# A graph network's edge counts: four fixed one-hots of a step from one interleaved comparison

## The chip, the cores and the metric

One core of one Trainium2 chip. The metric is the device time of one execution, in microseconds.

## The reference, cut to what matters

Four graph layers over 1250 nodes and 40000 edges, with 512 features. Each layer gathers features of source nodes and sums them per destination. The first one is

```python
i, j = edge_index[0], edge_index[1]
agg = jax.ops.segment_sum(x[j], i, num_segments=x.shape[0])
h = (1.0 + eps) * x + agg
h = jax.nn.relu(h @ W1.T + b1)
```

The others are attention over the edges (softmax per destination), a weighted message layer and a mean layer. All of them use the same edges, so the kernel turns the edge list once into dense 1250 x 1250 matrices: how often an edge joins two nodes, and the sums of the edge weights (in three bfloat16 parts). This is the edge build.

## The kernel before, in words

**Edges.** The sorted edges lie as 320 chunks of 125 (one edge per partition). `dst_oh` holds for every chunk a stationary matrix 125 x 128, bfloat16: 32 columns of one-hots of (quarter of the source, place in a window of eight destinations), and three copies of them times the weight's parts. It is made once, by 32 comparisons (L1164) and three multiplications of 10240 values by a repeated row (L1194). The moving matrix of a step is a one-hot of the source within its quarter: 313 columns, made on VectorE and multiplied on TensorE (L620); the products add up in PSUM.

**Groups.** There are 160 half windows `h` of eight destinations, four to a group `w`, so 40 groups; a group has four PSUM banks, and two groups alternate. Every half window gets FIX = 2 fixed steps per group, and in between as many late steps as its edges need: a hardware loop on VectorE and on TensorE whose count and first chunk come from a table (`groups_of`, L300: register loads, once per LOADS = 4 groups, on each of the two engines). The table gives group 0 a long loop and most of the later groups one trip.

**VectorE (L1232 to L1260).** Per group: `fixed(w, 0)`, the late loop, `fixed(w, 1)`. Each fixed call makes four one-hots (L1237), each a tensor_scalar comparison of `iota` (314 values, float16) with one float32 key per partition, and counts `base_oh` after each. Fixed slots of two groups alternate; it waits for `base_used` of the group two back. A late comparison (L1255) has one slot per half window and waits for `late_used` of the trip before.

**TensorE (L611 to L640).** Per group: four fixed products `base(0, h)`, each behind its own `base_oh`; the late loop, four products a trip; four of `base(1, h)`. Before a group it waits until ScalarE has evicted the group two back (`win_free`).

**ScalarE (L1593 to L1606)** copies each pair of banks into one of four window buffers in X, and in between computes degrees (L1584), the scaled features and, after window 50, `high_part(0)`, the rounded part of feature block 0 (L1591). **SP** stores each window with two DMAs (L398) and loads finished tiles of the counts back (L407, L409); it issues in order. The last windows come behind the loads of tiles before them.

**GpSimd (L1814 to L1836).** It clears the gaps of the window buffers, then makes `h_lo[0]`, the low part of feature block 0 (L1820, nine tiles in one tensor_tensor and the tenth in another), as soon as ScalarE's high part is there. Behind it come clears for the heavy rows (L1824 to L1827), which wait for all fixed products, and gathers (L1831), which wait for row numbers from VectorE (L1287).

**After the build** TensorE multiplies the features by the counts (L682, `aggregate`): per tile six products, three with the high and three with the low part. Tile t of block 0 waits for the counts of tile t; the loop starts behind `h_pool` 3, GpSimd's low part. VectorE makes the low parts of the other blocks (L1268).

Tiles share memory: the fixed and late one-hots lie in HT from word 0, `h_lo[0]` in HT from 3200 to 4480.

Of the kernel before, what the change touches and what calls it, by code (L numbers as in the profile page):

```python
# [19 lines left out]
F16 = mybir.dt.float16  # L20
BF16 = mybir.dt.bfloat16
# [3 lines left out]
P = 128  # L25
N, D, E = 1250, 512, 40000
T = -(-N // P)
# [7 lines left out]
FIX = 2  # L35
# [52 lines left out]
def rows(t):  # L88
    return min(P, N - t * P)


def constants():
    k1 = np.zeros((P, NK1 + 2 * NW + NH), np.float32)
    k1[:, K_IDENT:K_IDENT + P] = np.eye(P)
    for h in range(2):
        k1[:, K_TLO + h] = np.arange(P) * WIN + h * SUB
        k1[:, K_THI + h] = np.arange(P) * WIN + h * SUB + SUB - 1
    k1[:, K_ONES:K_ONES + P] = 1.0
    for k in range(3):
        for q in range(FIX):  # L100
            k1[:, K_PICK + k * FIX + q] = np.arange(P) + k * P - q
    k2 = np.zeros((NW, NK2), np.float32)
    k2[:, K2_UP:K2_UP + NC] = np.arange(NC) + 1
    k2[:, K2_DOWN:K2_DOWN + NC] = NC - np.arange(NC)
    k2[:, K2_TRI:K2_TRI + NW] = np.triu(np.ones((NW, NW)))
    k1[:, NK1:NK1 + 2 * NW] = np.arange(2 * NW) * KEY
    kh = k1[:, NK1 + 2 * NW:]
    kh[:, H_TRI:H_TRI + P] = np.triu(np.ones((P, P)), 1)
    kh[:, H_BEFORE:H_BEFORE + T * T] = np.tril(np.ones((T, T)), -1).reshape(-1)
    kh[:, H_SLOT:H_SLOT + SLOTS_H] = np.arange(SLOTS_H) + 1  # L110
    kh[:, H_ROW:H_ROW + T] = np.arange(P)[:, None] + np.arange(T) * P - OUTSIDE
    kh[:, H_OFF:H_OFF + 4] = np.arange(4) * T * P + OUTSIDE
    kh[:, H_OFF + 4] = OUTSIDE
    iota = np.broadcast_to(np.arange(HOT, dtype=np.float16), (P, HOT)).copy()
    return k1, k2, iota


def build(nc, A, out):
# [7 lines left out]
    with ExitStack() as ctx:  # L126
# [5 lines left out]
        def sem(name):  # L132
            if name not in sems:
                sems[name] = ctx.enter_context(nc.semaphore(name))
            return sems[name]
# [85 lines left out]
        epsI = BC[:, 1536:1536 + P]  # L221
        late_oh = src_oh[:, 2 * BASES:, :]
        winbuf = [X[:, :, :].rearrange("p t o -> p (t o)")[:, q * GH * PITCH:(q + 1) * GH * PITCH] for q in range(WB_N)]
        key_base = HT[:, 4860:4860 + 2 * NW]
# [24 lines left out]
        KC = [min(P, NC - k * P) for k in range(3)]  # L249
        base_key = BC[0:EC, W0:W0 + FIX * 2 * NW].rearrange("p (q v) -> p q v", q=FIX)  # L250

# [72 lines left out]

        def base_slot(w, i):
            return w % 2 * BASES + i

        def build_bank(w):
# [32 lines left out]
        def _(sp):  # L361
# [19 lines left out]
            load_last_x("x_in2")  # L381
            sp.dma_start(iota, A["iota"]).then_inc(sem("x_in"), 16)
            sp.dma_start(key_base, A["k1"][:, NK1:NK1 + 2 * NW]).then_inc(sem("x_in"), 16)
# [3 lines left out]
            for k in range(2):  # L387
                sp.dma_start(bias_col[:, 7 + k:8 + k], A["L2_bm"][k * P:(k + 1) * P].rearrange("(p o) -> p o", o=1))\
                    .then_inc(sem("x_in"), 16)

            def move_window(w):
# [123 lines left out]
        def _(pe):  # L515
# [95 lines left out]
            for w in range(NG):  # L611
# [10 lines left out]
                def base(q, h):  # L622
                    i = q * GH + h
                    pe.wait_ge(sem("base_oh"), BASES * w + i + 1)
                    step(h, dst_oh[0:EC, :, fixed_chunk(d[h], n0, q)][:, :, 0], src_oh[:, base_slot(w, i), 0:QUART],
                         q == 0).then_inc(sem("base_used"), 1)
# [59 lines left out]
            pe.wait_ge(sem("win_free"), NW - 2)  # L686
            pe.wait_ge(sem("h_pool"), 3)
            for t in range(T - 1):
                pe.wait_ge(sem("c_in%d" % (t % 2)), 32 * (t // 2 + 1))
                aggregate(0, t)  # L690
# [414 lines left out]
        def _(dve):  # L1105
# [100 lines left out]
            dve.wait_ge(sem("setup_ps"), 8)  # L1206
            dve.wait_ge(sem("x_in"), 7 * 16)
            for q in range(FIX):
# [23 lines left out]
            def fixed(w, q):  # L1232
                if w >= 2:
                    dve.wait_ge(sem("base_used"), BASES * (w - 2) + (q + 1) * GH)
                for h in range(GH):
                    v = GH * w + h
                    ve.tensor_scalar(src_oh[:, base_slot(w, q * GH + h), :], iota[0:EC, :], base_key[:, q, v:v + 1], None,  # L1237
                                     ALU.is_equal).then_inc(sem("base_oh"), 1)

# [32 lines left out]
            dve.wait_ge(sem("deg"), T)  # L1272
            dve.wait_ge(sem("x_in"), 8 * 16)
            link(ve.tensor_scalar(flag, deg[:, :], HEAVY, None, ALU.is_gt))
# [524 lines left out]
        def _(pool):  # L1799
# [18 lines left out]
            pool.wait_ge(sem("h_hi"), 2)  # L1818
            for t0, t1, n in ((0, T - 1, P), (T - 1, T, rows(T - 1))):
                gp.tensor_tensor(h_lo[0][0:n, t0:t1, :], H[0:n, t0:t1, 0:P], h_hi[0][0:n, t0:t1, :], ALU.subtract)\  # L1820
                    .then_inc(sem("h_pool"), 1)

# [15 lines left out]
            pool.wait_ge(sem("bc_in"), 48)  # L1838
            pool.wait_ge(sem("x_in"), 8 * 16 + 32)
            shift_and_add("l0", bc0[:, 2, :], ybuf)  # L1840
# [84 lines left out]
```

## Time and profile before

| | us |
|---|---|
| median of 3 runs | 1091.19 |
| lowest, highest | 1090.15, 1091.4 |
| the profiled execution's own time | 1088.51 |
| its span | 1086.7 |

| engine | busy us | share of the span |
|---|---|---|
| TensorE, products | 1011.2 | 93% |
| TensorE, weight loads | 686.8 | 63% |
| VectorE | 588.5 | 54% |
| ScalarE | 449.9 | 41% |
| GpSimd | 171.1 | 16% |

The mean granted TensorE clock is 0.981 of 2.4 GHz. In what follows a time in the trace is counted from the start of the span; a matmul's end is modelled, so starts are compared. A timeline merges neighbours of one line into a row: start, length from the first start to the last end, number. In brackets stands how long the engine had been idle before, and what ended it.

### The profile page before, as it was taken

Reading aid. Unit: us, or ns where it says so; the run is one execution under the profiler, and the core shown is the slowest. Engines: PE = TensorE matmul, PEld = TensorE weight load, DVE = VectorE, ACT = ScalarE, POOL = GpSimd, SP = SyncE. Lnnn points to the kernel's source line nnn. Section 1 sums busy time; section 2 is a strip of 40 time slices with the busy share of each in tenths; the row PEclk is TensorE's granted clock in tenths of the full one; section 3 lists DMA queues with packets and bytes.
Section 4 is the critical chain, followed back from the end, with each engine's and each line's share of the span. In section 5 each row is a group of like instructions: output and inputs, shape, how many; then the busy total and the mean of one; then the engine's idle time right before and its main releaser. Section 6 shows DMA issues by size and latency. Waiting matters only on the chain.

```text
span 1086.7 us, 17102 instructions
## 1 busy us (share of the span) xinstructions
PE 1011.2 (93%) x5898; PEld 686.8 (63%) x5898; DVE 588.5 (54%) x1700; ACT 449.9 (41%) x773; POOL 171.1 (16%) x194
## 2 busy tenths in 40 slices
PE   6977877899989999999999999999998998999998
PEld 3455655688544554788888888864457995555443
DVE  6878889922974011676676676646355248100133
ACT  5611465543545001666666666643346226300000
POOL 0000001012053000333333100026445020000000
PEclk9999987899999999999999999999999999999999
DMA  6003588884100001544554300071001070100011
GB/s 176 1 0 88 179 268 275 256 294 149 39 1 1 20 19 40 166 144 142 154 156 133 97 2 1 2 297 44 1 0 49 2 237 1 39 1 0 20 39 36
DMA packets 74682, 96.91 MB, mean 89 GB/s; under 512 B 7375, under 2 KB 63510, under 8 KB 74606
## 3 DMA queue, kind: packets, MB, share of 16 engines
q1 hardware_dynamic: 74446, 95.89, 27.8%
q8 instruction: 48, 0.79, 0.3%
q14 instruction: 28, 0.23, 0.1%
q0 software_dynamic: 160, 0.00, 0.0%
HBM read 58.24 MB, written 37.73 MB: 88 GB/s over the span
## 4 chain that ended last, share of the span: by engine, by line
PE 78%; DVE 10%; issue 7%; ACT 4%; DVEq 1%; DMA 0%; SPq 0%; ACTq 0%
PE PS L904 8%; PE PS L921 8%; PE PS L872 8%; PE PS L1065 8%; PE PS L620 7%; PE PS L1100 6%; PE PS L841 5%; PE PS L740 4%; PE PS L592 3%; PE PS L682 3%; DVE HT L1237 3%; PE PS L827 2%; PE PS L1020 2%; PE PS L1047 2%; DVE HT L1255 2%
## 5 line engine op out<-in xcount | busy, mean ns | idle before, releaser
L620 PE MATMUL PS<-HT,R 125*128 125x313 bf16 x636 | 129.5, 348 | 34.4 <-DVE HT L1237 14.8
L1375 DVE CUSTOM_DVE_ANT_0 HT<-PS,CD 128x1250 f32<-128x1250 f32 (+1 forms) x80 | 116.4, 1455 | 62.6 <-issue 62.6
L620 PEld LDWEIGHTS PS<-HT,R 125*128 x636 | 95.6, 172 | 68.8 <-issue 57.1
L1718 ACT ACTIVATE HT<-HT,soft 128x1250 f32<-128x1250 f32 (+1 forms) x80 | 107.2, 1340 | 10.4 <-DVE soft L1378 3.1
L1698 ACT COPY R<-PS 128x512 f32<-128x512 f32 (+1 forms) x120 | 64.5, 572 | 96.0 <-PE PS L904 96.0
L904 PE MATMUL PS<-K,HT 128*128 128x128 f32 (+2 forms) x800 | 102.1, 275 | 1.8 <-ACT HT L1718 0.8
L872 PE MATMUL PS<-R 64*128 64x512 f32 (+3 forms) x480 | 94.8, 526 | 3.1 <-DVE soft L1375 3.1
L904 PEld LDWEIGHTS PS<-K,HT 128*128 128x128 f32 (+2 forms) x800 | 84.7, 140 | 17.3 <-issue 14.6
L921 PE MATMUL PS<-R 128*64 128x128 f32 (+2 forms) x1600 | 94.2, 273 | 0.1
L1599 ACT COPY X<-PS 128x626 f32<-128x626 f32 x80 | 52.2, 693 | 96.0 <-PE PS L620 96.0
L1255 DVE TENSOR_SCALAR HT<-BC 125x314 bf16<-125x314 f16 x316 | 78.2, 310 | 23.2 <-PE PS L620 17.0
L921 PEld LDWEIGHTS PS<-R 128*64 128x64 f32 (+1 forms) x1600 | 84.8, 137 | 6.6 <-issue 5.8
L1065 PE MATMUL PS<-R,H 128*128 128x512 f32 (+2 forms) x240 | 85.2, 513 | 0.0
L872 PEld LDWEIGHTS PS<-R 64*128 64x128 f32 (+1 forms) x480 | 60.7, 183 | 30.7 <-issue 22.0
L1496 DVE SCALAR_TENSOR_TENSOR R<-PS,invdeg,BC 128x512 f32<-128x512 f32 (+1 forms) x10 | 7.5, 750 | 133.0 <-PE PS L1100 133.0
L1386 DVE COPY R<-PS 128x512 f32<-128x512 f32 (+1 forms) x80 | 54.3, 679 | 37.8 <-PE PS L904 37.3
L1237 DVE TENSOR_SCALAR HT<-BC 125x314 bf16<-125x314 f16 x320 | 71.8, 301 | 0.0
L1065 PEld LDWEIGHTS PS<-R,H 128*128 128x128 f32 (+1 forms) x240 | 45.0, 189 | 38.7 <-issue 38.5
L841 PE MATMUL PS<-HT,R 128*128 128x512 f32 (+1 forms) x192 | 67.4, 513 | 0.8 <-ACT HT L1648 0.8
L1558 ACT ACTIVATE rs<-mv,gate 128x1 f32<-128x1 f32 x70 | 20.6, 294 | 113.7 <-DVE mv L1216 113.6
L841 PEld LDWEIGHTS PS<-HT,R 128*128 128x128 f32 x192 | 36.4, 190 | 31.6 <-issue 31.5
L1354 DVE COPY R<-PS 128x1250 f32<-128x1250 f32 x4 | 5.8, 1460 | 66.2 <-PE PS L841 66.2
(254 smaller groups left out, 1484.6 us busy)
## 6 DMA issues: line engine op xcount, KB each, us to landing
edge_parts<-X SPq DMA_DIRECT2D x160, 160.0 KB, 2.8
R<-edge_parts SPq DMA_DIRECT2D x60, 156.5 KB, 2.4
CD<-edge_sums SPq DMA_DIRECT2D x1, 6250.0 KB, 21.7
counts_r<-edge_parts SPq DMA_DIRECT2D x10, 469.5 KB, 3.9
BC<-edge_parts SPq DMA_DIRECT2D x30, 156.5 KB, 2.4
CD<-edge_parts SPq DMA_DIRECT2D x3, 1565.0 KB, 12.5
edge_sums<-R SPq DMA_DIRECT2D x20, 156.5 KB
R<-edge_parts SPq DMA_DIRECT2D x18, 155.5 KB, 2.4
```

The source lines that it names most:

```text
L620: return mm(bank(b0 + h, QUART), stat, hot, start=first, stop=True, skip_group_check=True)
L841: i = mm(bank(5 * m + j, sn), wqk[p % 2][:, m, k, :], ht[:, k, s0:s0 + sn], start=k == 0, stop=k == KF - 1)
L872: i = mm(PS[0:n, a * N + s0:a * N + s0 + sn], qT[a * DK:(a + 1) * DK, p, t * P:t * P + n], kT[a * DK:(a + 1) * DK, p, s0:s0 + sn], start=T ...
L904: m = nc.tensor.transpose(PS[0:rows(j), o:o + n], Pb[u % 2][a][0:n, j * P:j * P + rows(j)], ident[0:n, 0:n])
L921: m = mm(PS[a * DK:(a + 1) * DK, o:o + n], V[0:rows(j), j, (2 * p + a) * DK:(2 * p + a + 1) * DK], PT[c % RING][0:rows(j), (2 * jj + a) * ...
L1065: i = mm(bank(3 * (f % 2) + j, sn), H[0:rows(t), t, f * P:(f + 1) * P], cs[0:rows(t), t, s0:s0 + sn], start=t == 0, stop=t == T - 1)
L1100: i = mm(bank(b)[0:n], src[:, k, t * P:t * P + n], w[:, k, :], start=k == 0, stop=k == KF - 1)
L1237: ve.tensor_scalar(src_oh[:, base_slot(w, q * GH + h), :], iota[0:EC, :], base_key[:, q, v:v + 1], None, ALU.is_equal).then_inc(sem("base_ ...
L1255: ve.tensor_scalar(late_oh[:, h, :], iota[0:EC, :], KEY * v, key[:, late_chunk(d[h], m)], ALU.add, ALU.is_equal)\
L1375: ve.tensor_tensor_reduce(Pb[s][a][0:n], PS[0:n, a * N:(a + 1) * N], cd[0:n, t, :], 1.0, -3e38, ALU.add, ALU.max, soft[0:n, s, a:a + 1]).t ...
L1698: sc.copy(PT[c % RING].rearrange("p (j n) -> p j n", j=4)[:, :, 0:n], bank(PIECE_BANK[i]).rearrange("p (j n) -> p j n", j=4)[:, :, 0:n]).t ...
L1718: sc.activation(Pb[s][a][0:n], Pb[s][a][0:n], ACT.Exp, bias=soft[0:n, s, 2 + a:3 + a], accum_out=zsum[0:n, z + a:z + a + 1]).then_inc(sem( ...
```

## The change

The four one-hots of a fixed step are made by one tensor_tensor comparison. Its first operand is a new constant `iota4`, the column numbers 0 to 312, each four times (1252 values, float16), loaded by a DMA of its own to HT behind `setup_dve` 1. Its second operand are the four keys of the group, now float16, repeated for every column. The result is interleaved: column n of one-hot h lies at 4n + h. The product reads it with a stride of four values, and all four wait for the one count of `base_oh` (now 2 per group). Late steps stay as they are. Since `iota4` lies where tiles 5 to 9 of `h_lo[0]` go, GpSimd makes tiles 0 to 4 as before and the rest only when all fixed comparisons are done; TensorE waits for the rest at tile 5 of block 0.

```diff
@@ constants
-    iota = np.broadcast_to(np.arange(HOT, dtype=np.float16), (P, HOT)).copy()
+    columns = np.concatenate([np.arange(HOT), np.repeat(np.arange(QUART), GH)])
+    iota = np.broadcast_to(columns.astype(np.float16), (P, HOT + GH * QUART)).copy()
@@ tiles
+        base4 = HT[0:EC, 0:2 * FIX * GH * QUART // 2].bitcast(BF16).rearrange("p (b n h) -> p b n h", n=QUART, h=GH)
+        iota4 = HT[0:EC, 3840:3840 + GH * QUART // 2].bitcast(F16).rearrange("p (n h) -> p n h", h=GH)
-        base_key = BC[0:EC, W0:W0 + FIX * 2 * NW].rearrange("p (q v) -> p q v", q=FIX)
+        base_key = BC[0:EC, W0:W0 + FIX * NW].bitcast(F16).rearrange("p (q v) -> p q v", q=FIX)
@@ SP
-            sp.dma_start(iota, A["iota"]).then_inc(sem("x_in"), 16)
+            sp.dma_start(iota, A["iota"][:, 0:HOT]).then_inc(sem("x_in"), 16)
...
+            sp.wait_ge(sem("setup_dve"), 1)
+            sp.dma_start(iota4.rearrange("p n h -> p (n h)"), A["iota"][0:EC, HOT:]).then_inc(sem("x_in"), 16)
@@ TensorE
                 def base(q, h):
                     i = q * GH + h
-                    pe.wait_ge(sem("base_oh"), BASES * w + i + 1)
-                    step(h, dst_oh[0:EC, :, fixed_chunk(d[h], n0, q)][:, :, 0], src_oh[:, base_slot(w, i), 0:QUART],
+                    pe.wait_ge(sem("base_oh"), FIX * w + q + 1)
+                    step(h, dst_oh[0:EC, :, fixed_chunk(d[h], n0, q)][:, :, 0], base4[:, w % 2 * FIX + q, :, h],
                          q == 0).then_inc(sem("base_used"), 1)
...
-            pe.wait_ge(sem("h_pool"), 3)
+            pe.wait_ge(sem("h_pool"), 2)
             for t in range(T - 1):
+                if t == T // 2:
+                    pe.wait_ge(sem("h_pool"), 3)
@@ VectorE
-                for h in range(GH):
-                    v = GH * w + h
-                    ve.tensor_scalar(src_oh[:, base_slot(w, q * GH + h), :], iota[0:EC, :], base_key[:, q, v:v + 1], None,
-                                     ALU.is_equal).then_inc(sem("base_oh"), 1)
+                keys = base_key[:, q, GH * w:GH * (w + 1)].unsqueeze(1).to_broadcast([EC, QUART, GH])
+                ve.tensor_tensor(base4[:, w % 2 * FIX + q, :, :], iota4, keys, ALU.is_equal).then_inc(sem("base_oh"), 1)
@@ GpSimd
-            for t0, t1, n in ((0, T - 1, P), (T - 1, T, rows(T - 1))):
-                gp.tensor_tensor(h_lo[0][0:n, t0:t1, :], H[0:n, t0:t1, 0:P], h_hi[0][0:n, t0:t1, :], ALU.subtract)\
-                    .then_inc(sem("h_pool"), 1)
+            def low_part_0(t0, t1, n):
+                return gp.tensor_tensor(h_lo[0][0:n, t0:t1, :], H[0:n, t0:t1, 0:P], h_hi[0][0:n, t0:t1, :], ALU.subtract)
+
+            low_part_0(0, T // 2, P).then_inc(sem("h_pool"), 1)
+            pool.wait_ge(sem("base_oh"), FIX * NG)
+            low_part_0(T // 2, T - 1, P)
+            low_part_0(T - 1, T, rows(T - 1)).then_inc(sem("h_pool"), 1)
```

The other waits on `x_in` count one load more.

## Rows read from the trace of the kernel before

**Rows 1.** The page, part 4: the chain that ended last.

```profile
PE 78%; DVE 10%; issue 7%; ACT 4%; DVEq 1%; DMA 0%; SPq 0%; ACTq 0%
```

**Rows 2.** The same chain from 50 to 225 us, shares by line.

```profile
by line: PE PS L620 44.5%; DVE HT L1237 16.0%; issue 14.4%; DVE HT L1255 11.8%; PE PS L592 4.4%; PE PS L682 2.0%; DVEq L300 1.9%; DVEq L1251 1.9%; DVEq L1255 1.5%; ACT X L1599 1.1%; ACT H L1576 0.4%; PE PS L582 0.2%
```

**Rows 3.** Busy time in three stretches, each a quad of groups.

```profile
core 0: us, PE busy (x) PEld busy (x) DVE busy (x) ACT busy (x) POOL busy (x), PEclk, DMA share, GB/s
135.40:146.00 10.60, 8.58 (x46) 6.42 (x47) 10.31 (x50) 6.89 (x11) 0.00 (x0) 1.00 0.91 281
170.80:185.50 14.70, 10.44 (x52) 7.55 (x52) 13.51 (x49) 9.10 (x16) 3.42 (x2) 0.85 0.86 266
185.50:196.90 11.40, 9.72 (x49) 7.26 (x50) 10.49 (x49) 5.85 (x10) 0.00 (x0) 0.74 0.76 234
```

**Rows 4.** VectorE's timeline: a run of fixed comparisons, and late ones after a stall.

```profile
126.09 0.94 DVE L1255 TENSOR_SCALAR HT<-BC 125x314 bf16<-125x314 f16 x4 [1.80 <-PE PS L620]
...
153.67 1.04 DVE L1255 TENSOR_SCALAR HT<-BC 125x314 bf16<-125x314 f16 x4 [0.33 <-PE PS L620]
...
166.32 1.08 DVE L1255 TENSOR_SCALAR HT<-BC 125x314 bf16<-125x314 f16 x4 [0.28 <-PE PS L620]
...
175.56 1.08 DVE L1255 TENSOR_SCALAR HT<-BC 125x314 bf16<-125x314 f16 x4 [0.40 <-PE PS L620]
...
187.21 1.77 DVE L1237 TENSOR_SCALAR HT<-BC 125x314 bf16<-125x314 f16 x8
189.89 1.08 DVE L1255 TENSOR_SCALAR HT<-BC 125x314 bf16<-125x314 f16 x4 [0.91 <-PE PS L620]
...
204.07 1.09 DVE L1255 TENSOR_SCALAR HT<-BC 125x314 bf16<-125x314 f16 x4 [0.43 <-PE PS L620]
...
213.54 1.08 DVE L1255 TENSOR_SCALAR HT<-BC 125x314 bf16<-125x314 f16 x4 [0.84 <-PE PS L620]
```

**Rows 5.** TensorE's timeline from 185 us: products of the build.

```profile
188.18 9.37 PE L620 MATMUL PS<-HT,R 125*128 125x313 bf16 x48 [1.55 <-DVE HT L1237]
199.73 1.53 PE L620 MATMUL PS<-HT,R 125*128 125x313 bf16 x8 [2.18 <-DVE HT L1237]
```

**Rows 6.** The register loads of line 300 on TensorE's sequencer: ns min, median, max.

```profile
L300 PEldq TENSOR_LOAD <-BC x10: 1545/2002/2562, 52.3 to 208.9; - x10
```

**Rows 7.** TensorE's timeline and line 620: the first eight products, and all (ns min/median/max).

```profile
57.59 1.25 PE L620 MATMUL PS<-HT,R 125*128 125x313 bf16 x8
...
L620 PE MATMUL PS<-HT,R x636: 294/304/512, 57.6 to 221.2; 125*128 125x313 bf16 x159
```

**Rows 8.** Busy time in a stretch at half clock (columns as in rows 3).

```profile
161.47:165.70 4.23, 4.23 (x17) 2.89 (x18) 2.76 (x13) 1.27 (x2) 0.00 (x0) 0.50 0.92 306
```

**Rows 9.** VectorE before and in the build: durations, timeline, groups by form.

```profile
L1237 DVE TENSOR_SCALAR HT<-BC x320: 245/299/318, 52.6 to 220.6; 125x314 bf16<-125x314 f16 x160
...
40.72 10.88 DVE L1194 TENSOR_TENSOR R<-R,BC 125x10240 bf16<-125x10240 bf16 x2
...
L1178 DVE TENSOR_TENSOR HT<-HT,BC 125x320 f32<-125x320 f32 x1 | 0.5, 493 | 0.0
...
L1161 DVE TENSOR_TENSOR CD<-CD 80x2 f32<-80x2 f32 x1 | 0.2, 157 | 0.0
```

**Rows 10.** GpSimd's low part and VectorE's batch at the same moment, timeline.

```profile
181.03 3.42 POOL L1820 TENSOR_TENSOR h_lo<-H,h_hi 128x1152 fp32r<-128x1152 f32 x2 [128.92 <-ACT h_hi L1591]
...
181.03 3.73 DVE L1255 TENSOR_SCALAR HT<-BC 125x314 bf16<-125x314 f16 x4
```

**Rows 11.** SP's timeline: its issues of DMAs late in the build.

```profile
185.61 9.94 SPq L398 DMA_DIRECT2D edge_parts<-X  x12
...
212.09 10.86 SPq L398 DMA_DIRECT2D edge_parts<-X  x16
223.12 0.46 SPq L407 DMA_DIRECT2D counts_r<-edge_parts  x1
```

**Rows 12.** After the build: the chain, and ScalarE's wait for the counts of tile 8.

```profile
221.51 10.46 PE PS L682 x54
...
227.71 1.25 ACT L1584 ACTIVATE WA<-counts_r 128x1250 bf16<-128x1250 f32 x1 [2.69 <-DMA counts_r<-edge_parts]
```

More of the change, by code:

```diff
@@ L323, in agg_bank @@
             return ((4, 5, 6), (0, 1, 2), (3, 7, 6), (0, 1, 2))[f][j]
-        def base_slot(w, i):
-            return w % 2 * BASES + i
         def build_bank(w):
@@ L1206, in _ @@
             dve.wait_ge(sem("setup_ps"), 8)
-            dve.wait_ge(sem("x_in"), 7 * 16)
+            dve.wait_ge(sem("x_in"), 8 * 16)
             for q in range(FIX):
@@ L1272, in _ @@
             dve.wait_ge(sem("deg"), T)
-            dve.wait_ge(sem("x_in"), 8 * 16)
+            dve.wait_ge(sem("x_in"), 9 * 16)
             link(ve.tensor_scalar(flag, deg[:, :], HEAVY, None, ALU.is_gt))
@@ L1838, in _ @@
             pool.wait_ge(sem("bc_in"), 48)
-            pool.wait_ge(sem("x_in"), 8 * 16 + 32)
+            pool.wait_ge(sem("x_in"), 9 * 16 + 32)
             shift_and_add("l0", bc0[:, 2, :], ybuf)
```

## The prediction

> **What bounds the kernel now.** I read the page first: the chain that ended last is 78% TensorE and 10% VectorE [rows 1]. Then the same chain for the stretch of the edge build alone, 50 to 225 us: there line 620 (the products) holds 44.5%, the two comparisons on VectorE (lines 1237 and 1255) 28% together, and "issue" 14.4% [rows 2]. So the build is a duet: no engine is busy all the time, and it must be seen which of the two paces which part.
>
> I call the four one-hots of one step a batch: F for a fixed step, L for a late one. A group has F, its late trips, F; a group of the long tail has one trip, so F L F. Four groups share one load of registers (a quad). The windows by quad show VectorE busy 10.31 of 10.6, 13.51 of 14.7 and 10.49 of 11.4 us, TensorE 8.58, 10.44 and 9.72 [rows 3]. The timeline of VectorE shows why: it runs comparison after comparison and stops once or twice in a quad, at an L that waits for TensorE to give back its single late slot: at 189.89 for 0.91 us, and in the other quads of the tail last at 126.09, 153.67, 166.32, 175.56, 204.07 and 213.54 [rows 4]. TensorE's timeline shows the other half: 48 products in one run, then an idle of 1.55, 2.18 us [rows 5]. This is the register load ahead of the quad, 2.0 us in the middle and 2.6 at most [rows 6]. While TensorE loads, VectorE runs ahead by F, L, F, F and stops. Once the first L is used, VectorE never stops again and TensorE follows it to the end of the quad. So of the 12 batches of a quad only those after the last stall are on the path; those before it lie beside the register load.
>
> **TensorE's own limit.** Eight products take 1.25 us, the last one 0.29 [rows 7]: (1.25 - 0.29) / 7 = 0.137 us from start to start at the full granted clock, 1.00 (2.4 GHz). At 0.50 (1.2 GHz) 17 start within 4.23 us, 0.26 each [rows 8]. At full clock a quad needs 48 x 0.137 + 2.1 = 8.7 us. The quad from 185.5 has a mean clock of 0.74 [rows 3], so 0.52 x 11.4 = 5.9 us at half clock; 1.6 of it is the idle load, and the other 4.3 do the work of 2.2. So it needs 8.7 + 2.1 = 10.8 against 11.4; where the clock is 0.85 some 10. There is room of 0.6 to 1 us.
>
> **The parts.** *F on VectorE.* Now: eight comparisons take 1.77 us, the last one 0.30 [rows 4, 9], so 0.21 from start to start and 0.84 a batch. After: one tensor_tensor of 1252 values. The nearest row is the multiplication of 16-bit values by a repeated row: two of 10240 in 10.88 us [rows 9]; less the 0.157 us that a tensor_tensor of two values takes [rows 9], 0.523 ns a value. So 1252 x 0.523 = 0.65, with 0.16 fixed 0.81 us long, and, with the 0.09 by which a comparison overlaps the next (0.30 - 0.21), 0.72 from start to start. Gain 0.12 a batch. Bounds: the keys are read as runs of four, which no row shows; above, the pace of the 32-bit row (rival 4); below, nothing faster than 1252 x 0.523 without any fixed part, 0.65. I take 0.72, since type, operation class and repeated operand are those of the row.
>
> The Trainium skill speaks against this: by VectorE: DVE Perf Modes, section on the perf-mode tier table, tensor_scalar goes at four 16-bit values a cycle and tensor_tensor at two only. With the cycle table of that page (section on the TRN2 errata) a batch would go from 0.57 to 0.71 us, an estimate, and the sum to a loss. The trace disagrees on the first figure: four cost 0.84 [rows 4].
>
> How many F are on the path: after the last stall I count 7 in the quad of 126.09, 5 in the next (which starts without one; the five after its first late step), 3 at 153.67, 3 at 166.32, 5 at 175.56, 5 at 189.89, 3 at 204.07, 5 at 213.54: 36. 36 x 0.12 = 4.3 us. In the quads with several trips (up to 122 us) each second trip waits for TensorE, which now gets the F ahead of it all at once, so what VectorE gains there TensorE takes longer for: nothing. The long loop of group 0 has no F in it: nothing.
>
> *The wait.* All four products of a batch now wait for the whole comparison. The last product could start 3 x 0.21 + 0.30 = 0.93 after the batch began; now at 0.81 + 3 x 0.137 = 1.22: 0.29 later. Within a quad this is only lag. At its end it delays the register load, but that load needs the products handed over, not done; I take half, 0.15, in 8 quads: 1.2 us lost. VectorE part: 4.3 - 1.2 = 3.1.
>
> *Product reads every fourth value.* No row shows a strided moving operand. Bounds: 0.137 us a product, as now, and the 0.26 of the half-clock row as the nearest slower pace. I take 0.137: the same instruction reads its stationary operand at a stride of 320 values already, and the counts products stream 4-byte values, twice the bytes. The Trainium skill, SBUF — State Buffer (the box on cachelines), gives reads that hit each 16-byte line twice full speed; a stride of 8 bytes does. No row here shows it.
>
> *GpSimd.* Its low part runs at 181.03 for 3.42 us, and the VectorE batch that starts at that moment takes 3.73 instead of 0.94 [rows 4, 10]: 2.8 us lost in the quad of 14.7 us. Five of the ten tiles stay there, 1.7 us; the loss is halved: 1.4 gained. The other five tiles (1.7 us) go behind the last F. TensorE reads them at tile 5 of the counts products: 54 products of nine tiles take 10.46 us, 1.16 a tile [rows 12], so 5.8 us after it starts. Cover 4 us; if it were gone, at most 1.7. GpSimd's clears, queued behind, come 1.7 us later; the gathers after them wait for VectorE's row numbers, which need the ranks that TensorE makes after tile 5 of the next feature block. Nothing.
>
> *The extra load on SP.* One issue of 0.68 us (10.86 / 16, [rows 11]) and 313 KB. VectorE asks for it only behind the multiplications that end at 51.6 [rows 9]. The wait ahead of it (setup_dve 1) has only the window stores behind it on SP, which need an evicted group. Nothing. The narrower key subtraction and the smaller count of semaphores: nothing.
>
> *What is late next.* SP issues the stores without a gap at the end: 16 in 10.86 us, then the next counts at 223.12 [rows 11], 12.1 us a quad, more than the 11.4 us that the engines need. The counts of tile 8 land for ScalarE at about 227.6 [rows 12]; TensorE wants them 8 x 1.16 = 9.3 us after 221.5, at 230.8. Slack 3.2 us, and SP moves up too by its own idle time: 12 issues in 9.94 us from 185.61 [rows 11] hold 1.8 us. Together 5.0 us, near the gain. I take 0.3 off.
>
> **Sum.** 3.1 + 1.4 - 0.3 = 4.2 us. After the build TensorE runs on without a gap through the counts products [rows 12], so the rest shifts. The profiled execution took 1088.51 us (span 1086.7); it would be 1084.3. The median of the runs, 1091.19, is 2.7 above the profiled one; from it I forecast 1087.0.
>
> **Rivals.** 1 (forecast): gains between 2.2 and 7 us, 0.60. This kernel's runs can tell about 0.2% from no change, 2.2 us.
> 2: the gain is covered. If TensorE's register load and half-clock stretches (or SP's issue pace) end last in most quads, only GpSimd's 1.4 us and a part of the rest is left: 1089.0 to 1091, say 1090. For it: SP's 12.1 us a quad, and TensorE's room of 0.6 to 1 us. Against: VectorE runs without stalls for most of each quad. 0.24.
> 3, the other side: the strided read is slow. At 0.26 us a product, F costs TensorE 1.05: a quad needs 8 x 1.05 + 4 x 0.55 + 2.1 = 12.7 us against 11.4, plus 1.3 in nine quads, 12 less 1.4: about 1101. It decides from (11.4 - 2.1 - 2.2) / 8 = 0.89 a batch, 0.22 us a product. 0.10.
> 4: the comparison does not keep the pace of the 16-bit row. The 32-bit row of 320 values takes 0.493 us [rows 9], (493 - 157) / 320 = 1.05 ns a value: 1252 x 1.05 + 0.16 = 1.47 us long, 1.38 from start to start; a quad needs 8 x 1.38 + 4 x 0.84 = 14.4, 3 more in ten: 1121. 0.04. A milder form: were the new batch 0.14 dearer than four comparisons, 36 x 0.14 + 1.2 - 1.4 = 4.8 us more, 1096; since four measure 0.84, 0.02. (The page on the perf modes, above, gives this 0.14.)
>
> **Numbers.** Faster 0.60; within 0.2% 0.24; slower 0.16. The range goes from a gain of 7 (fixed part gone from F, GpSimd's stall gone, a half-clock stretch fewer) to 0.8 above the time before, where rival 2 ends: 1084.2 to 1092.0. It leaves out rivals 3 and 4.
>
> **What the profile would show.** Line of the fixed comparison: 80 instructions near 0.81 us. Right if quads of the tail are 0.4 to 0.6 us shorter, VectorE's stall near GpSimd's tensor_tensor is about 1.4 us, and TensorE starts the counts products near 217. Wrong if products of line 620 start further apart than 0.14 us inside an F, if the comparison takes over 1.3 us, if TensorE waits for counts at tile 8, or if quads stay at 11.4 us with VectorE idle longer.

## The result and the profile after

| | us |
|---|---|
| before, median of 5 runs on the same chip | 1091.19 (1088.19 to 1092.89) |
| after, median of 5 runs | 1100.18 (1097.57 to 1102.19) |
| ratio, with its 95% interval | 1.0084 [1.0061, 1.0107] |
| the profiled execution after, its span | 1100.18, 1098.4 |

The change makes the kernel 9 us slower; 1087.0 was forecast. The page after: its first line, the line that answers to [rows 1], and three groups of its part 5 (busy us, mean ns of one, idle before):

```profile
PE 1038.6 (95%) x5898; PEld 696.9 (63%) x5898; DVE 575.5 (52%) x1460; ACT 450.3 (41%) x773; POOL 170.9 (16%) x195
...
PE 82%; DVE 7%; issue 6%; ACT 4%; DMA 0%; DVEq 0%; SPq 0%; ACTq 0%
...
L622 PE MATMUL PS<-HT,R 125*128 125x313 bf16 x636 | 154.6, 401 | 19.9 <-DVE HT L1257 5.3
...
L1257 DVE TENSOR_SCALAR HT<-BC 125x314 bf16<-125x314 f16 x316 | 76.2, 305 | 43.3 <-PE PS L622 39.9
...
L1240 DVE TENSOR_TENSOR HT<-HT,BC 125x1252 bf16<-125x1252 f16 x80 | 61.2, 805 | 0.1
```

VectorE did what was promised: 805 ns a comparison (0.81 forecast), 61 us in all where the comparisons one by one took 71.8, and the engine is less busy than before (575.5 us against 588.5). The loss is on TensorE, 1038.6 us busy against 1011.2. The chain of the edge build alone (50 to 235 us, answering to [rows 2]) shows which part took over:

```profile
by line: PE PS L622 71.1%; issue 8.4%; DVE HT L1257 5.4%; DVE HT L1240 4.3%; PE PS L594 3.7%; ACT X L1601 2.8%; PE PS L684 2.1%; DVEq L1257 0.8%; DVEq L1253 0.6%; DVEq L303 0.4%; ACT H L1578 0.4%
```

The products go from 44.5% to 71.1% of this chain, the two comparisons from 28% to 10%. The duet has become a solo. The products' durations (ns min, median, max; answering to [rows 7]):

```profile
L622 PE MATMUL PS<-HT,R x636: 297/451/529, 56.7 to 230.7; 125*128 125x313 bf16 x159
```

TensorE's timeline over three quads of the tail, answering to [rows 5]:

```profile
181.00 11.88 PE L622 MATMUL PS<-HT,R 125*128 125x313 bf16 x48 [0.66 <-ACT X L1601]
194.71 12.03 PE L622 MATMUL PS<-HT,R 125*128 125x313 bf16 x48 [1.83 <-DVE HT L1240]
207.44 11.61 PE L622 MATMUL PS<-HT,R 125*128 125x313 bf16 x48 [0.71 <-DVE HT L1240]
```

VectorE's, answering to [rows 4]:

```profile
185.49 0.94 DVE L1257 TENSOR_SCALAR HT<-BC 125x314 bf16<-125x314 f16 x4 [0.45 <-PE PS L622]
186.34 1.52 DVE L1240 TENSOR_TENSOR HT<-HT,BC 125x1252 bf16<-125x1252 f16 x2
188.35 2.28 DVE L1257 TENSOR_SCALAR HT<-BC 125x314 bf16<-125x314 f16 x4 [0.48 <-PE PS L622]
...
196.36 0.94 DVE L1257 TENSOR_SCALAR HT<-BC 125x314 bf16<-125x314 f16 x4 [2.01 <-PE PS L622]
...
199.32 1.09 DVE L1257 TENSOR_SCALAR HT<-BC 125x314 bf16<-125x314 f16 x4 [0.59 <-PE PS L622]
...
202.51 0.94 DVE L1257 TENSOR_SCALAR HT<-BC 125x314 bf16<-125x314 f16 x4 [0.59 <-PE PS L622]
...
209.12 0.95 DVE L1257 TENSOR_SCALAR HT<-BC 125x314 bf16<-125x314 f16 x4 [1.40 <-PE PS L622]
```

48 products take 11.6 to 12.0 us where they took 9.4 to 9.7, and VectorE, which stopped once or twice a quad, now stops ahead of nearly every late batch. The idle of TensorE between quads has shrunk instead: 0.66 and 0.71 us, where 1.55 and 2.18 stood, and 1.83 only behind the batch that GpSimd slows down (188.35). While TensorE loads the next quad's registers it still has a backlog to stream: in six quads eight products start within the load, where one or two did before. The waits between 60 and 231 us, after (us in total, times, longest):

```profile
DVE HT L1257 <- PE PS L622: 36.0, 50, 3.3
PE PS L622 <- DVE HT L1257: 5.1, 21, 0.3
PE PS L622 <- DVE HT L1240: 5.0, 10, 1.8
```

and the same view of the kernel before:

```profile
PE PS L620 <- DVE HT L1237: 14.8, 8, 2.6
DVE HT L1255 <- PE PS L620: 13.7, 35, 1.8
PE PS L620 <- DVE HT L1255: 9.2, 28, 1.3
```

The groups by line from 56 to 232 us give the balance; TensorE's products after and, below, before:

```profile
L622 PE MATMUL PS<-HT,R 125*128 125x313 bf16 x636 | 154.6, 401 | 19.9 <-DVE HT L1257 5.3 <-DVE HT L1240 5.0 <-ACT X L1601 4.7
```

```profile
L620 PE MATMUL PS<-HT,R 125*128 125x313 bf16 x636 | 129.5, 348 | 34.4 <-DVE HT L1237 14.8 <-DVE HT L1255 9.3 <-ACT X L1599 4.9
```

25.1 us more busy, 14.5 less idle: 10.6. The build ran from 57.59 to 221.51 and now runs from 56.68 to 231.18, which is 10.6 us longer. Single executions of one kernel differ by some 3 us either way, more than half of it by how long TensorE's clock stands at 0.50 (1.2 GHz), so I take medians for totals and profiles for places.

The clock also hides a part of the loss. In the five runs after the change its mean is 0.984 to 0.990; in the 42 runs of the kernel before that stand beside the experiments it is 0.973 to 0.984, and among these 0.001 less goes with some 0.65 us more. By that estimate the change would lose some 5 us more at the old clock. What raised the clock is open. The kernel before takes the same time on this chip as on the two of the experiments, which speaks against the chip; e6 below reads at a stride too and has 0.975 to 0.981, which speaks against the stride.

Two forecasts about neighbours can be read here too. GpSimd's second half, and ScalarE at tile 8 of the counts:

```profile
228.69 1.73 POOL L1822 TENSOR_TENSOR h_lo<-H,h_hi 128x512 fp32r<-128x512 f32 x2 [38.60 <-DVE HT L1240]
```

```profile
235.67 1.25 ACT L1586 ACTIVATE WA<-counts_r 128x1250 bf16<-128x1250 f32 x1 [1.26 <-DMA counts_r<-edge_parts]
```

The half is done at 230.4, before the counts products even begin; and ScalarE gets the counts 4.5 us after the end of the build where it got them 6.2 after it, since the longer build left SP more time.

### The profile page after: what moved, and what is told of

Its sections match the earlier page's. It is cut to its first block, busy times and chain, and to the rows that moved or that the text cites. A ratio compares the mean times of both kernels' runs of the same rounds, so it can differ in the third digit from the quotient of the medians.

```text
span 1098.4 us, 16865 instructions
## 1 busy us (share of the span) xinstructions
PE 1038.6 (95%) x5898; PEld 696.9 (63%) x5898; DVE 575.5 (52%) x1460; ACT 450.3 (41%) x773; POOL 170.9 (16%) x195
## 4 chain that ended last, share of the span: by engine, by line
PE 82%; DVE 7%; issue 6%; ACT 4%; DMA 0%; DVEq 0%; SPq 0%; ACTq 0%
PE PS L622 12%; PE PS L908 8%; PE PS L925 8%; PE PS L876 8%; PE PS L1069 8%; PE PS L1104 6%; PE PS L845 5%; PE PS L744 4%; PE PS L594 3%; PE PS L684 3%; PE PS L831 2%; PE PS L1024 2%; PE PS L1051 2%; PE PS L782 2%; PE PS L769 2%
## 5 line engine op out<-in xcount | busy, mean ns | idle before, releaser
L622 PE MATMUL PS<-HT,R 125*128 125x313 bf16 x636 | 154.6, 401 | 19.9 <-DVE HT L1257 5.3
L622 PEld LDWEIGHTS PS<-HT,R 125*128 x636 | 103.2, 174 | 71.4 <-issue 37.9
L876 PE MATMUL PS<-R 64*128 64x512 f32 (+3 forms) x480 | 97.0, 537 | 3.1 <-DVE soft L1377 3.1
L1257 DVE TENSOR_SCALAR HT<-BC 125x314 bf16<-125x314 f16 x316 | 76.2, 305 | 43.3 <-PE PS L622 39.9
L1240 DVE TENSOR_TENSOR HT<-HT,BC 125x1252 bf16<-125x1252 f16 x80 | 61.2, 805 | 0.1
L831 PE MATMUL PS<-WA,HT 128*128 128x512 f32 (+1 forms) x80 | 37.7, 618 | 3.9 <-ACT HT L1650 3.9
```

Of the source, the lines that this page charges most:

```text
L622: return mm(bank(b0 + h, QUART), stat, hot, start=first, stop=True, skip_group_check=True)
L876: i = mm(PS[0:n, a * N + s0:a * N + s0 + sn], qT[a * DK:(a + 1) * DK, p, t * P:t * P + n], kT[a * DK:(a + 1) * DK, p, s0:s0 + sn], start=T ...
L1240: ve.tensor_tensor(base4[:, w % 2 * FIX + q, :, :], iota4, keys, ALU.is_equal).then_inc(sem("base_oh"), 1)
L1257: ve.tensor_scalar(late_oh[:, h, :], iota[0:EC, :], KEY * v, key[:, late_chunk(d[h], m)], ALU.add, ALU.is_equal)\
```

## The experiments

Seven kernels, in two sets; each set shares one chip and its runs of the kernel before. The open questions: how much of the 9 us is the stride of the product's read, how much the coarser wait and the new comparison, what GpSimd's split gives alone, and why a VectorE that now has time to spare brought nothing.

**e1: the change with products that read neighbouring values.** Only the addresses differ; same comparison, same wait.

```diff
-                    step(h, ..., base4[:, w % 2 * FIX + q, :, h],
+                    step(h, ..., base_flat[:, w % 2 * FIX + q, (QUART - 1) * h:(QUART - 1) * h + QUART],
```

> The changed kernel with one edit: each fixed product reads 313 neighbouring values of the interleaved slot instead of every fourth. The comparison, its one wait for four products, the key layout and GpSimd's split stay. The sums of the fixed steps are wrong in this kernel: it takes the wrong one-hot columns. Theory S (the strided read is slow): fixed products start 0.14 us apart as before instead of 0.285, TensorE waits for VectorE again in each quad, and the time is that of my prediction's sum, 1086 to 1089 us. Rival W (the pace comes from the one wait for a whole batch, behind which the four weight loads stand in line): products stay 0.28 apart and the time near 1100. If the pace is 0.14 but the time above 1091, something else than the read was lost as well.

Measured: 1092.31 us (median of 10), before 1091.05 (of 25 in this set), ratio 1.002 [1.0006, 1.0034]. By the medians the stride costs 7.9 us of the 9, with some 2 us of noise either way. The products' durations, then TensorE's timeline in a tail quad:

```profile
L623 PE MATMUL PS<-HT,R x636: 294/302/511, 57.4 to 219.5; 125*128 125x313 bf16 x159
```

```profile
187.00 9.56 PE L623 MATMUL PS<-HT,R 125*128 125x313 bf16 x48 [1.99 <-DVE HT L1241]
```

Median back to 302 ns, the quad to 9.56 us. The pace is that of theory S, the time is not: 1086 to 1089 were expected. Comparison, wait and split together lose 1.3 us by the medians (2.2 by the ratio) where 4.2 were to be gained.

**e2: a ruler for the stride.** The eight fixed products of a group read another tile at steps of 1, 2, 3, 4, 6, 8, 16 and 32 values; the late ones stay as they are.

```diff
+        strided = {s: flat[:, 0:QUART * s].rearrange("p (n s) -> p n s", s=s)[:, :, 0] for s in (1, 2, 3, 4, 6, 8, 16, 32)}
-                    step(h, ..., base4[:, w % 2 * FIX + q, :, h],
+                    step(h, ..., strided[(1, 2, 3, 4, 6, 8, 16, 32)[i]],
```

> The changed kernel, but the eight fixed products of a group read their moving operand from the idle-standing memory of the stationary one-hots at a step of 1, 2, 3, 4, 6, 8, 16 and 32 values of two bytes; so the fixed steps add other numbers and the output is not the reference's. Only the pace of each is of interest. Theory S with a rule by bytes (the port gives four bytes a column at full rate, as the float32 operands have): step 1 and 2 at 0.14 us, 3 and above slower, 0.285 from step 4. Theory S with a rule by contiguity: step 1 at 0.14, all others at 0.285. A rule by lines of 16 bytes: 1 to 4 alike, 8 and above slower still; step 4 at 0.285 in the changed kernel already speaks against it. Theory W: all eight alike at 0.28.

Measured: 1119.11 us (one run; only the pace is read). The products that read the tile, then the late and last ones:

```profile
L624 PE MATMUL PS<-R x320: 302/522/763, 57.8 to 248.2; 125*128 125x313 bf16 x160
L624 PE MATMUL PS<-HT,R x316: 297/315/515, 58.5 to 246.6; 125*128 125x313 bf16 x158
```

From the starts in the trace, sorted by step, median over the groups at full granted clock:

```
step, values of 2 bytes          1      2      3      4      6      8      16     32
us from start to the next start  0.152  0.151  0.213  0.272  0.407  0.559  0.568  0.528
us long (the record)             0.314  0.312  0.378  0.452  0.587  0.738  0.747  0.705
```

(Late products of this kernel: 0.139 from start to start.) A step of 2 costs nothing beside a step of 1. From there the product costs about 0.068 us for each value of step up to 8, that is 16 bytes, and no more beyond. At 313 columns the plateau of 0.56 us is 1.8 ns a column. This fits a price of 1.8 ns for each new stretch of 16 bytes, hidden as long as the columns themselves take longer: a step of 2 crosses 78 stretches (0.14 us), 3 crosses 117 (0.21), 4 crosses 157 (0.28), 6 crosses 235 (0.42). The expectation had spoken against such a rule, as a step of 4 was slow already; the table has it. That 32 is cheaper than 16 the rule does not explain.

**e3: two one-hots interleaved, not four**, for a step of 2 and a wait for pairs; the rest as in the change.

```diff
+PAIR = 2
-                    pe.wait_ge(sem("base_oh"), FIX * w + q + 1)
-                    step(h, ..., base4[:, w % 2 * FIX + q, :, h],
+                    pe.wait_ge(sem("base_oh"), (FIX * w + q) * GH // PAIR + h // PAIR + 1)
+                    step(h, ..., base2[:, (w % 2 * FIX + q) * GH // PAIR + h // PAIR, :, h % PAIR],
...
+                for g in range(GH // PAIR):
+                    v = GH * w + PAIR * g
+                    keys = base_key[:, q, v:v + PAIR].unsqueeze(1).to_broadcast([EC, QUART, PAIR])
+                    ve.tensor_tensor(base2[:, (w % 2 * FIX + q) * GH // PAIR + g, :, :], iota2, keys, ALU.is_equal)\
+                        .then_inc(sem("base_oh"), 1)
```

> The changed kernel with two one-hots interleaved instead of four: two comparisons of 626 values a batch, each waited for by its two products, read at every second value. All of the computation is there. VectorE: 626 x 0.523 + 157 = 0.48 us long, 0.40 from start to start, 0.80 a batch against 0.84 before and 0.72 now. If step 2 reads at full rate (by bytes): products 0.14 apart, TensorE out of the way, and a gain of about 36 x 0.04 + 1.4 for GpSimd = 3 us, 1088. If step 2 is as slow as step 4: near 1100 as the changed kernel. Theory W gives a value between, as the wait is for two products.

Measured: 1090.52 us (of 10), ratio 0.9994 [0.9977, 1.0011]. VectorE's fixed comparison between 60 and 215 us:

```profile
L1243 DVE TENSOR_TENSOR HT<-HT,BC 125x626 bf16<-125x626 f16 x151 | 63.0, 481 | 0.6 <-PE PS L623 0.5
```

Products start 0.150 us apart: in the whole kernel too, a step of 2 is almost free (0.137 without a step). The gain of 3 us that was expected did not come: the kernel is level with the one before. It is 1.8 us below e1, barely clear of the noise; wait, comparison and step all differ from e1, and the wait is the only one of them that got cheaper.

**e4: GpSimd's split alone**, in the kernel before (its diff is the GpSimd part of the change, with the two waits on `h_pool`, and the wait for all fixed comparisons counts eight a group).

```diff
+            low_part_0(0, T // 2, P).then_inc(sem("h_pool"), 1)
+            pool.wait_ge(sem("base_oh"), BASES * NG)
+            low_part_0(T // 2, T - 1, P)
+            low_part_0(T - 1, T, rows(T - 1)).then_inc(sem("h_pool"), 1)
```

> The kernel before with GpSimd's part of the change alone: tiles 0 to 4 of the low part of block 0 during the build, the rest behind the last fixed comparison, TensorE waits for it at tile 5. My prediction's term: VectorE's batch at that moment takes 2.4 us instead of 3.7 and 1.4 us are gained, 1089.8. Rival: the quad with the stall is paced by TensorE and SP all the same, or the later tiles are waited for at tile 5: no gain, 1090.5 to 1092.

Measured: 1089.48 us (of 10), ratio 0.9979 [0.9963, 0.9995], the fastest kernel of the study. GpSimd's first half and the batch of VectorE beside it, timelines:

```profile
178.08 1.69 POOL L1822 TENSOR_TENSOR h_lo<-H,h_hi 128x640 fp32r<-128x640 f32 x1 [126.70 <-ACT h_hi L1593]
```

```profile
177.94 2.35 DVE L1257 TENSOR_SCALAR HT<-BC 125x314 bf16<-125x314 f16 x4
```

The batch takes 2.35 us where it took 3.73 [rows 10]: 1.4 less, as worked out. The median gains 1.6, by the interval between 0.5 and 4; the profiled execution is the fastest of the ten.

**e5: the coarse wait alone**, in the kernel before: each fixed product waits for all four comparisons of its step.

```diff
-                    pe.wait_ge(sem("base_oh"), BASES * w + i + 1)
+                    pe.wait_ge(sem("base_oh"), BASES * w + (q + 1) * GH)
```

> The kernel before with one edit: each of the four fixed products of a batch waits for all four comparisons of the batch. Comparisons, layout and GpSimd are as before. It asks what the coarse wait alone costs. The first run without the strided read lost 0.35 us in each of the eight groups with several trips and gained nothing in the tail; theory L (the lag of the whole batch in front of a late loop, whose second trip waits for TensorE): the same here, here even a little more, since four comparisons end 0.93 us after the start instead of 0.80: 3 to 4 us over the kernel before, 1094 to 1095, and the stall of the late comparison on TensorE longer by 0.4 us in groups 1 to 8. My prediction's step (nothing lost there, 0.15 in each of eight quads of the tail): 1.2 us, 1092.

Measured: 1097.83 us (of 6), before 1090.53 (of 17 in this set), ratio 1.0073 [1.005, 1.0096]. More than expected. Part of TensorE's timeline in the groups with two late trips:

```profile
116.32 0.94 PE L620 MATMUL PS<-HT,R 125*128 125x313 bf16 x4 [0.26 <-DVE HT L1255]
117.73 0.79 PE L620 MATMUL PS<-HT,R 125*128 125x313 bf16 x4 [0.47 <-DVE HT L1237]
118.83 1.50 PE L620 MATMUL PS<-HT,R 125*128 125x313 bf16 x8 [0.30 <-issue]
120.60 0.92 PE L620 MATMUL PS<-HT,R 125*128 125x313 bf16 x4 [0.27 <-DVE HT L1255]
121.99 0.78 PE L620 MATMUL PS<-HT,R 125*128 125x313 bf16 x4 [0.47 <-DVE HT L1237]
```

In each of the two groups shown TensorE stands 0.47 us for a fixed batch. The kernel before has no such row in its groups with two trips, two rows of which are

```profile
113.73 3.38 PE L620 MATMUL PS<-HT,R 125*128 125x313 bf16 x16 [0.30 <-DVE HT L1255]
117.41 3.32 PE L620 MATMUL PS<-HT,R 125*128 125x313 bf16 x16 [0.29 <-issue]
```

Its idle there is 0.28 to 0.35 us, none of it for a fixed batch.

**e6: e5 with products that read every fourth value** of the four slots. The old comparisons, the stride's price by itself.

```diff
+        base_int = HT[0:EC, 0:2 * BASES * HOT // 2].bitcast(BF16).rearrange("p (b n h) -> p b n h", n=HOT, h=GH)
-                    step(h, ..., src_oh[:, base_slot(w, i), 0:QUART],
+                    step(h, ..., base_int[:, w % 2 * FIX + q, 0:QUART, h],
```

> The one-wait kernel with fixed products that read every fourth value over the four slots of their batch, so the fixed steps add other columns and the output is not the reference's; the comparisons stay four of the old kind. If the stride costs the same without the new comparison, products start 0.285 us apart in fixed batches and the time is 8 to 10 us over the one-wait kernel: 1102 to 1104. If the slow pace needed the new comparison beside it (both reading the same lines), it stays 0.14 to 0.17 and the time does not move.

Measured: 1107.12 us (of 4), ratio 1.015 [1.0122, 1.0179]: 9.3 us over e5. The products' durations:

```profile
L621 PE MATMUL PS<-HT,R x636: 297/460/522, 57.4 to 238.0; 125*128 125x313 bf16 x159
```

So the slow pace needs neither the new comparison nor what it wrote, and the stride's price, 7.9 and 9.3 us, is the same within the noise.

**e7: a faster VectorE and nothing else.** In the kernel before the fixed comparisons write 8 columns instead of 314 from group 2 on; the products still read all 313.

```diff
-                    ve.tensor_scalar(src_oh[:, base_slot(w, q * GH + h), :], iota[0:EC, :], base_key[:, q, v:v + 1], None,
+                    n = HOT if w < 2 else 8
+                    ve.tensor_scalar(src_oh[:, base_slot(w, q * GH + h), 0:n], iota[0:EC, 0:n], base_key[:, q, v:v + 1], None,
```

> The kernel before, but from group 2 on a fixed comparison writes only 8 of its 314 columns, so that VectorE's work for them shrinks and the sums of the fixed steps are of stale one-hots. It asks whether VectorE paces the tail at all, as my prediction had it. A short comparison goes some 0.08 us quicker from start to start, 0.3 us a batch, more than twice what the change could give. Theory V (VectorE paces): 36 x 0.3 = 11 us gained, 1080, quads of the tail near 10 us. Theory T (TensorE's own sequence of twelve products a group, 9.4 us a quad whatever VectorE does, and the register load of 2 us behind it): quads stay at 11.2 to 11.6 us, 1 to 3 us gained in all, 1088 to 1090.

Measured: 1089.69 us (of 10), ratio 0.9995 [0.9974, 1.0016]: no gain. Busy time from 126 to 220 us (columns as in [rows 3]), before and then e7:

```profile
126.00:220.00 94.00, 75.44 (x377) 56.33 (x375) 85.76 (x377) 53.78 (x86) 3.42 (x2) 0.84 0.83 258
```

```profile
126.00:220.00 94.00, 75.57 (x376) 56.55 (x376) 67.06 (x380) 53.70 (x86) 3.08 (x2) 0.84 0.84 258
```

Timelines of e7, VectorE and then TensorE, and one of its waits from 60 to 231 us:

```profile
201.77 1.14 DVE L1238 TENSOR_SCALAR HT<-BC 125x8 bf16<-125x8 f16 x8
```

```profile
163.67 9.55 PE L620 MATMUL PS<-HT,R 125*128 125x313 bf16 x48 [2.07 <-DVE HT L1238]
...
188.00 9.37 PE L620 MATMUL PS<-HT,R 125*128 125x313 bf16 x48 [2.20 <-DVE HT L1238]
199.64 9.59 PE L620 MATMUL PS<-HT,R 125*128 125x313 bf16 x48 [2.27 <-DVE HT L1238]
```

```profile
DVE HT L1256 <- PE PS L620: 28.3, 40, 2.7
```

VectorE does the same number of comparisons in 67.1 us instead of 85.8 (eight take 1.14 us, not 1.77), and TensorE does the same number of products in the same time, at the same clock. The time saved is waited away: 28.3 us instead of 13.7. In the tail it is TensorE that paces, but for the quad in which GpSimd holds VectorE up.

**The build in three parts**, from TensorE's starts (the last part to its last end) in each profile (us):

```
                    group 0   groups 1 to 8   groups 9 to 39   clock at 0.50 in the build
before              29.74     41.41           92.77            30.7
e4 split            29.74     40.58           89.35            13.7
e7 fast VectorE     29.74     41.28           92.66            34.1
e5 coarse wait      30.37     46.87           93.23            34.1
e1 contiguous       30.08     43.57           88.81            20.5
e3 pairs            29.91     42.31           90.61            30.7
after               30.98     48.16           95.36            10.2
e6 wait and stride  31.11     50.45           99.54            37.5
```

Each row is one execution and holds its own half-clock stretches. So here are four groups with several trips that ran at full clock in all four kernels below (us from the group's first product to the next group's):

```
                    group 1   group 2   group 5   group 6
before              7.22      5.93      3.66      3.62
e5 coarse wait      7.68      6.55      4.28      4.23
e1 contiguous       7.43      6.28      4.01      3.98
after               7.96      6.89      4.62      4.60
```

The coarse wait costs 0.58 us a group, the coarse wait with the new comparison 0.32, and the stride 0.59 on top of that. (0.1 us of e5's group 5 is at half clock.)

## Why the prediction was wrong

***Product reads every fourth value* is the step that failed.** It gave 0.137 us a product, with 0.26 as the upper bound. Measured are 0.285 us at full clock, outside even the bound (e6 and the changed kernel alike; 466 ns long against 300). 320 products x 0.148 are 47 us of TensorE work. Of it 7.9 us show in the time by the change less e1 (9.3 by e6 less e5); the rest took the place of idle time: the waits for VectorE, and the register loads between quads, now beside a backlog. The two arguments for 0.137 fell with it. That the *stationary* operand is read at a stride says nothing of the moving one; and the counts products' 4-byte values are neighbours, 4 bytes from column to column, which in e2's bfloat16 products is the last free distance.

The Trainium skill, SBUF — State Buffer (the box on cachelines), which I put beside this step, gives full speed to reads that hit each 16-byte line twice. For this operand the measurement decides otherwise: a step of 4 hits each line twice and costs twice as much; four hits (a step of 2) are free. The box's 16 bytes are seen all the same, in the plateau from a step of 8 on.

***TensorE's own limit* was wrong too**, and it would have sunk the gain without any stride. I took 0.137 us, the pace of products that are already waiting, for all 48 of a quad, and found room of 0.6 to 1 us. The medians from start to start at full clock in the tail (groups 9 to 39), by place in the batch, show what is paid between them:

```
                      F, to its 2nd  2nd to 3rd  3rd to 4th  4th to the next batch
before, F ahead of L  0.213          0.142       0.138       0.208
before, late batch    0.215          0.138       0.138       0.326
before, F behind L    0.213          0.138       0.137       0.234
e7, F ahead of L      0.212          0.143       0.138       0.206
e7, late batch        0.214          0.137       0.138       0.343
e7, F behind L        0.215          0.138       0.137       0.234
```

The last column leaves out the register loads. The rows of the kernel before sum to 2.3 us a group, 9.4 a quad, as the quads that run through show, and with the 2.0 us of register load a quad is 11.4 us: the period measured before. VectorE's long rows without a stall, on which I counted 36 F as on the path, were those of an engine just keeping up. e7 tests it: its comparisons start (1.14 - 0.22) / 7 = 0.13 us apart, 0.08 less than before, so 0.32 a batch and by my count 36 x 0.32 = 11 us. The interval of its ratio allows 2.8 us of gain at most. The tail of e1 (88.81 us) is near that of e4 (89.35) for the same reason. So with products that read neighbours the gain would not have come either (e1: 1092.3): the condition of rival 2, that the gain on VectorE is covered, held, and the loss by the wait came on top. What makes the first and the last product of a batch slower than the two between them was not taken apart; the late batch's 0.33 has the end of the hardware loop in it.

***F on VectorE*: the size right, the place wrong.** 805 ns long and 1.52 us for two, 0.72 from start to start as given; the runs of four keys and the new operation kept the pace of the 16-bit row. The Trainium skill, VectorE: DVE Perf Modes, would have had the old batch at 0.57 us and so the new one dearer; the trace had 0.84, and 0.72 for the new one stands. e7 shows where the old batch's time lies: 8 values take 223 ns and 314 values 299, so 306 values more cost only 76 ns, 0.25 ns each, against 0.523 in the new comparison. The one large comparison pays more per value and the fixed part once. But the 4.3 us did not come, since in the tail it gained on the wrong engine, and *multi-trip groups: nothing* was wrong by sign. There the late loop goes back and forth between the engines, and the fixed batches stand in that path. At full clock e5 pays 0.58 us a group; the new comparison gives back 2 x 0.12 of it, which leaves 0.34, and e1 shows 0.32. (Over groups 1 to 8 e5's profile is 5.5 us longer, but 2.4 of it lie in groups 4 and 8, which e5 ran at half clock almost throughout.) With the stride the change pays another 4.6 us there (48.16 against 43.57), and 0.9 in group 0.

***The wait* was too small.** 1.2 us, for the tail. In the tail it costs nothing that can be seen (e5: 93.23 against 92.77, with 21.3 us of it at half clock against 28.6), as TensorE has the batches ahead of it; in groups 0 to 8, which the step left out, it costs 6.1 in e5's profile, of which some 5 would be left at full clock (8 x 0.58, and 0.6 in group 0).

**Right:** *GpSimd* (1.4 us; VectorE's batch 2.28 where 3.73 stood, e4 1.6 us faster), its later tiles covered, *the extra load on SP* nothing. *What is late next* could not be tested by the change, whose build became longer, but e4's profile tests it. There the build ends 5 us earlier, and the counts products still run through, though the counts of tile 8 reach ScalarE 2.4 us later after the end of the build than before:

```profile
216.54 10.55 PE PS L682 x54
```

```profile
225.12 1.25 ACT L1586 ACTIVATE WA<-counts_r 128x1250 bf16<-128x1250 f32 x1 [5.07 <-DMA counts_r<-edge_parts]
```

TensorE wants them at 216.5 + 9.3 = 225.8: the slack is used up but for 0.7 us, near the 0.3 us of loss that the forecast took at that gain.

**The sum, by medians:** split -1.6 (e4), comparison with its wait +2.8 (e1 less e4), stride +7.9 (the change less e1): +9.1. Each term is a step from one kernel to the next, so that they add up to the 9.0 measured is no test of them; e6 less e5, +9.3, is the second measurement of the stride. Each carries some 2 us of noise, and the change less e1 also the difference in clock. Rival 3 named the cause, a point of decision at 0.22 us and 1101 us; it had 0.10. Its 1101 was partly luck: it reckoned with 0.26 us a product, not 0.285, and put all of the cost on nine quads. Against e1 the build is 12.0 us longer in the profiles (the whole spans differ by 9.2), 6.5 in the tail, where part of it goes into the idle time between quads, and 5.5 in groups 0 to 8. I gave it so little for a weak reason: no row showed a strided moving operand, and I let a page and a look-alike row fill the gap.

## What to carry to other kernels

Count the bytes from one column of a matmul's moving operand to the next: in these products of 313 bfloat16 columns up to 4 were free, at 8 the product took twice as long, at 16 and more four times. An interleaving that saves the writer 0.12 us a batch can so cost the reader 0.6. And who paces a duet is not told by the engine that shows no idle: take the follower's pace from batches that it gets one at a time, with what stands between them, or shorten the leader's work in one run (e7) before rewriting it. A wait made coarser cost nothing that could be seen where the consumer had a backlog, and 0.3 us a batch where the two engines hand work back and forth. Before two profiles are compared stretch by stretch, see where each stood at half clock: 2.4 of e5's 5.5 us lay in two such groups. Of all versions the kernel before with GpSimd's operation split in two is the best, 0.2% faster (0.05 to 0.4%): an operation that holds up another engine can be cut, and its later part put where nobody is waiting.

## What the runs showed of the hardware that was not expected

- The price of a step in the moving operand: 0.15, 0.15, 0.21, 0.27, 0.41, 0.56, 0.57, 0.53 us for 313 columns at steps of 1, 2, 3, 4, 6, 8, 16, 32 two-byte values; a step of 32 is a little cheaper than 16.
- It hardly depends on TensorE's clock: with a step of 4, products start 0.285 us apart at full clock and 0.287 at the granted 0.50 (e6), while contiguous ones go from 0.137 to 0.261. This speaks against the columns themselves as what takes the time.
- VectorE's tensor_scalar of 8 values takes 223 ns, of 314 values 299 ns (from start to start 0.13 and 0.21 us): so three quarters of the long one's time would be there for hardly any values.
- Four tensor_scalar comparisons that take 0.94 us take 3.73 us beside a GpSimd tensor_tensor of 3.42 us, and 2.35 beside one of 1.69.
